# The experts stage of a four-layer kernel: last token group written out, end of the last unit reordered, two GpSimd steps moved

## The reference, cut to what matters

```python
logits = einsum('bsh,eh->bse', x, classifier_w)
probs  = softmax(logits)
idx    = top_k(probs + bias, 2);  rw = probs[idx] * 1.5
g = einsum('bsh,eih->bsei', x, gate_w)
u = einsum('bsh,eih->bsei', x, up_w)
act = silu(g) * u
out = einsum('bse,bseh->bsh', w_full[..., :8], einsum('bsei,ehi->bseh', act, down_w))
out = out + x * sum(w_full[..., 8:], axis=-1)
```

## Time and profile before

| | |
|---|---|
| median of 3 runs | 836.54 us |
| lowest and highest | 835.28 and 837.89 us |
| span of the profiled execution, first to last instruction | 832.7 us |
| that execution's own time | not given apart from its span; the median of the runs is 3.8 us above the span |
| first matmul of the experts' units, and first of the latent stage | 172.0 and 349.2 us |
| busy share of the span, TensorE, VectorE, ScalarE, GpSimd | 90%, 74%, 49%, 69% |

### The profile page before, as it was taken

The page is one execution under the profiler, slowest core; times in us unless marked ns, Lnnn a source line. Parts: engine busy times, 40 slices in busy tenths (PEclk is TensorE's granted clock), DMA queues, the critical chain, the costliest instruction groups (busy, mean ns, idle before and its releaser), DMA issues. The chain is left out here.

```text
span 832.7 us, 14911 instructions
## 1 busy us (share of the span) xinstructions
PE 750.6 (90%) x4808; PEld 535.8 (64%) x4808; DVE 615.8 (74%) x1115; ACT 406.6 (49%) x1084; POOL 570.9 (69%) x589
## 2 busy tenths in 40 slices
PE   4999999859999999689999999999999999866785
PEld 2555555447878877556777777777777777543454
DVE  5898999868887878665565576886678667749995
ACT  1688888533322322216454544555454445444453
POOL 5667776326676757564657778787878887716976
PEclk9999999989999999999999999999999999998999
DMA  9200000040000010122110000000000000000011
GB/s 262 103 1 0 0 0 1 2 168 20 20 19 20 19 57 0 57 95 96 48 49 1 1 1 1 3 1 1 1 1 2 1 2 1 1 2 7 25 33 38
DMA packets 8763, 24.12 MB, mean 29 GB/s; under 512 B 1711, under 2 KB 5167, under 8 KB 8087
## 3 DMA queue, kind: packets, MB, share of 16 engines
q1 hardware_dynamic: 8154, 23.28, 8.5%
q10 hardware_dynamic: 549, 0.08, 0.1%
HBM read 21.26 MB, written 2.10 MB: 28 GB/s over the span
## 5 line engine op out<-in xcount | busy, mean ns | idle before, releaser
L1606 POOL TENSOR_TENSOR q<-turned 64x512 f32<-64x512 f32 x128 | 168.0, 1313 | 23.5 <-DVE turned L1532 9.5
L1283 PE MATMUL ps<-l_yt,a 128*128 128x512 f32 x576 | 144.1, 400 | 2.1 <-ACT p L1429 1.6
L1283 PEld LDWEIGHTS ps<-l_yt,a 128*128 128x128 f32 x576 | 104.9, 188 | 26.9 <-issue 4.7
L1593 POOL TENSOR_TENSOR p<-p,l_inverse 128x512 f32<-128x512 f32 x64 | 66.8, 1047 | 77.3 <-DVE l_inverse L1554 76.9
L1429 ACT ACTIVATE p<-ps,l_negmax 128x128 f32<-128x128 f32 x256 | 91.1, 382 | 43.1 <-DVE l_negmax L1523 43.1
L1532 DVE TENSOR_TENSOR turned<-ps,rope 128x1024 f32<-128x1024 f32 x64 | 78.0, 1220 | 42.4 <-PE ps L1283 39.8
L871 PE MATMUL ps<-yt_experts,wsplit 128*128 (+1 forms) x384 | 97.3, 403 | 5.7 <-DVE h L974 5.2
L467 DVE TENSOR_REDUCE negmax<-ps 128x4 f32<-128x512 f32 x128 | 84.4, 685 | 13.3 <-PE ps L290 12.8
L871 PEld LDWEIGHTS ps<-yt_experts,wsplit 128*128 128x128 f32 x384 | 71.2, 192 | 23.1 <-issue 5.4
L1523 DVE TENSOR_REDUCE l_negmax<-ps 128x4 f32<-128x512 f32 x64 | 41.2, 686 | 45.8 <-PE ps L1341 45.6
L383 ACT ACTIVATE pt<-ps 128x512 f32<-128x512 f32 x128 | 71.2, 599 | 6.8 <-PE ps L312 4.5
(11 more groups left out here) (213 smaller groups left out, 1571.1 us busy)
## 6 DMA issues: line engine op xcount, KB each, us to landing
wide<-in_wide SPq DMA_DIRECT2D x8, 768.0 KB, 4.5
mx_raw<-in_mx SPq DMA_DIRECT2D x8, 384.0 KB, 3.1
x<-in_x SPq DMA_DIRECT2D x4, 512.0 KB, 8.4
ctx_t<-in_ctx_t SPq DMA_DIRECT2D x1, 2048.0 KB, 7.8
out<-x SPq DMA_DIRECT2D x16, 128.0 KB, 1.7
narrow<-in_narrow SPq DMA_DIRECT2D x8, 192.0 KB, 2.7
ktraw<-in_ctx_rows SPq DMA_DIRECT2D x1, 1248.0 KB
wraw<-in_gate SPq DMA_DIRECT2D x1, 1024.0 KB, 18.1
```

The lines of the kernel that those rows point to most:

```text
L1283: out = pe.matmul(tile_bank(n, k), a[i][:, pa, kin, k * 128:(k + 1) * 128], yt[j % 2][:, py, kin, :, :].rearrange("p b s -> p (b s)"), sta ...
L1593: pool.tensor_tensor(p[:, head, :, :], p[:, head, :, :], spread(inverse[:, head, :], 2, S), ALU.mult).then_inc(normed[head], 1)
L1606: t = pool.tensor_tensor(out[rows[(head + half) % 2], head, :], turned[rows[head], half, :], turned[rows[head], 2 + half, :], ALU.add)
```

## The change

It writes the last group out as code, with a loop over groups 1 and 2 only. In step 31 VectorE weighs unit 31 (`weigh`) before it quantises the last chunk. GpSimd finishes the last chunk one step later, behind the low part of unit 31, and TensorE's transposes of it come a step later, behind the last down products. The offset of the rows moves from x = 7 to x = 5 in every group. The means and variances of 12 sequences move into step 29, between up and down. The reciprocal deviations of the first four sequences move into step 30, and the other twelve to the latent stage. One step at the end falls away.

```diff
             group(0)
-            with engine.Fori(1, GROUPS) as j:
+            with engine.Fori(1, GROUPS - 1) as j:
                 group(j)
-            for x in range(3):
+            group(GROUPS - 1)
+            for x in range(2):
                 step(UNITS + x, GROUPS, x)
...
-                if x % 2 == 0 and inside(u - 2, UNITS):
+                if x % 2 == 0 and inside(u - 2, UNITS) and inside(u, UNITS):
+                    turn_quantised(u, 4 * j + x // 2, x)
+                if isinstance(u, int) and u == UNITS + 1:
+                    turn_quantised(UNITS, 2 * EXPERTS, 0)
...
-                if inside(u - 1, UNITS):
-                    dve.wait_ge(weight_spread, u)
-                    dve.wait_ge(inner_made, u)
-                    wait(dve, h_lo, u - 2)
-                    dve.tensor_tensor(h[old][:, :], inner[old][:, :], weight_ps, ALU.mult).then_inc(h_made, 1)
+                if inside(u - 1, UNITS) and inside(u, UNITS):
+                    weigh(u - 1, old)
+                if isinstance(u, int) and u == UNITS - 1:
+                    weigh(u, par)
...
                     (shift_up if x % 2 else block_powers)(u, j, x)
+                if isinstance(u, int) and u == UNITS - 3:
+                    mean_and_variance(dve, m, parts_made, stats_made, range(B - 4))
                 if x == 1 and inside(j - 1, GROUPS):
-                    if not inside(j, GROUPS):
-                        mean_and_variance(dve, m, parts_made, stats_made, range(B - 4))
...
-                if inside(u, UNITS) and x == 7:
+                if inside(u, UNITS) and x == 5:
                     pool.wait_ge(affine, j + 4)
...
-                    else:
-                        pool.wait_ge(mx_step, MX_STEPS * (c + 1))
-                        wait(pool, mx_turned, c - 1)
-                        pool.tensor_tensor(quantised[(x // 2) % 2][:, :].rearrange("p (n c) -> p n c", c=MX), chunk,
-                                           spread(scale[:, :], 2, MX), ALU.mult).then_inc(mx_made, 1)
+                    elif not isinstance(u, int) or u < UNITS - 1:
+                        finish_chunk(c, x)
+                if isinstance(u, int) and u == UNITS:
+                    finish_chunk(2 * EXPERTS - 1, EXPERTS - 1)
...
-                if inside(u, UNITS) and x in (3, 7):
+                if inside(u, UNITS) and x in (3, 5):
                     scale_x(j, x)
+                if isinstance(u, int) and u == UNITS - 2:
+                    pool.wait_ge(stats_made, B - 4)
+                    reciprocal_deviation(pool, m, var_made, slice(0, 4))
...
             steps(pool, step)
-            pool.wait_ge(stats_made, B - 4)
-            reciprocal_deviation(pool, m, var_made, slice(0, B - 4))
...
-                    reciprocal_deviation(pool, m, var_made, slice(B - 4, B))
+                    reciprocal_deviation(pool, m, var_made, slice(4, B))
```

More of the change, by code:

```diff
@@ L898, in step, with turn_quantised @@
                     t.then_inc(down_made, 1)
-                if x % 2 == 0 and inside(u - 2, UNITS):
[L900 to L908, removed]
+                if x % 2 == 0 and inside(u - 2, UNITS) and inside(u, UNITS):
+                    turn_quantised(u, 4 * j + x // 2, x)
+                if isinstance(u, int) and u == UNITS + 1:
+                    turn_quantised(UNITS, 2 * EXPERTS, 0)
+            def turn_quantised(u, c, x):
+                pe.wait_ge(mx_made, c)
+                wait(pe, mx_kept, c - 1)
+                if isinstance(u, int) and u in (2, 4):
+                    pe.wait_ge(w_lo, 2 + u // 2)
+                for i in range(3):
+                    t = pe.transpose(mx_ps[:, i * 128:(i + 1) * 128],
+                                     quantised[(x // 2 - 1) % 2][:, i * 128:(i + 1) * 128], m.ident16[:, :])
+                t.then_inc(mx_turned, 1)
             for b in range(B):
@@ L995, in step, with weigh @@
                         dve.bn_stats(m.parts[:, 4 * (j - 1) + s, :], m.x[:, 4 * (j - 1) + s, :]).then_inc(parts_made, 1)
+            def weigh(u, par):
+                dve.wait_ge(weight_spread, u + 1)
+                dve.wait_ge(inner_made, u + 1)
+                wait(dve, h_lo, u - 1)
+                dve.tensor_tensor(h[par][:, :], inner[par][:, :], weight_ps, ALU.mult).then_inc(h_made, 1)
             def mx_then(instruction, c, k, before):
@@ L1079, in step, with finish_chunk @@
                         pool.tensor_tensor(chunk, chunk, spread(inverse[:, :], 2, MX), ALU.mult).then_inc(mx_divided, 1)
-                    else:
-                        pool.wait_ge(mx_step, MX_STEPS * (c + 1))
-                        wait(pool, mx_turned, c - 1)
-                        pool.tensor_tensor(quantised[(x // 2) % 2][:, :].rearrange("p (n c) -> p n c", c=MX), chunk,
-                                           spread(scale[:, :], 2, MX), ALU.mult).then_inc(mx_made, 1)
+                    elif not isinstance(u, int) or u < UNITS - 1:
+                        finish_chunk(c, x)
+                if isinstance(u, int) and u == UNITS:
+                    finish_chunk(2 * EXPERTS - 1, EXPERTS - 1)
                 if inside(u, UNITS) and x < ROTARY_STEPS:
                     rotate_context(pool, m, rotated, j, x)
-                if inside(u, UNITS) and x in (3, 7):
+                if inside(u, UNITS) and x in (3, 5):
                     scale_x(j, x)
+                if isinstance(u, int) and u == UNITS - 2:
+                    pool.wait_ge(stats_made, B - 4)
+                    reciprocal_deviation(pool, m, var_made, slice(0, 4))
+            def finish_chunk(c, x):
+                chunk = raw[(x // 4) % 2][:, (x // 2) % 2, :].rearrange("p (n c) -> p n c", c=MX)
+                pool.wait_ge(mx_step, MX_STEPS * (c + 1))
+                wait(pool, mx_turned, c - 1)
+                pool.tensor_tensor(quantised[(x // 2) % 2][:, :].rearrange("p (n c) -> p n c", c=MX), chunk,
+                                   spread(scale[:, :], 2, MX), ALU.mult).then_inc(mx_made, 1)
             steps(pool, step)
-            pool.wait_ge(stats_made, B - 4)
-            reciprocal_deviation(pool, m, var_made, slice(0, B - 4))
 def rotate_context(pool, m, rotated, j, k):
```

## The result

The kernel after takes 831.32 us, the median of 9 runs (829.22 to 836.05), against 837.45 for the kernel before in 9 runs beside it (835.28 to 839.90). The ratio is 0.9931 [0.9916, 0.9946], so the change makes the kernel faster by 0.7%.

A forecast was written before the change was run, and what follows sets the result against it. It took the stage's end to be a relay of single engines, and VectorE to be held by GpSimd in units 9 and 25. Terms -3.0 + 0.9 - 2.6 - 0.8 = -5.5 gave 831.0 us, range 829.0 to 834.8.

The forecast's parts named there:

- End of the stage, -3.0: End of experts stage: earlier weighting of unit 31 and no offset between last low parts, -3.0 us (bounds -3.4, -0.9).
- Means and variances, +0.9: Step 29: twelve VectorE instructions between up and down stand on the path without cover, +0.9 us (bound 0).
- Offset, -2.6: Units 9 and 25: with the offset at x = 5 VectorE is no longer held, -1.32 us each, -2.6 together.
- no operation of VectorE on operands in the same memory runs beside one of GpSimd: Experts stage: VectorE and GpSimd exclude each other on the same memory, and the one starting second waits.
- The rival with the moved offset: At x = 5 the offset delays the powers past `inner` of x = 7, +5.2 us over four groups; 838.8 us, chance 0.06.
- Last group written out, -0.8: Step 24 and units 25 and 29: no back edge or register work, -0.3, -0.3 and -0.2 us.
- Deviations, 0: Step 30 and latent stage: the split reciprocal deviations fit into GpSimd's idle time, 0 us, bound +0.3.
- The sum: All terms together: -5.5 us, giving 831.0 us; this case had chance 0.52.
- I take the same 3.8 around its span: Whole kernel: the runs' median lies 3.8 us above the profiled span, taken as the profiled execution's excess too.
- the forecast span, 827.2: Whole kernel: the profiled span expected after the change, beside a forecast time of 831.0 us.
- whatever ends the stage earlier moves all that follows by as much: End of experts stage: the latent stage's start waits for every engine, so an earlier end shifts everything after equally.
- 1.3 of scatter: Forecast range: allowance for scatter between runs below the lowest and above the highest of the first three cases.

The follow-up runs named there:

- putting the offset back: Kernel after with the offset of the rows returned to x = 7 in groups 0 to 2, group 3 keeping x = 5; 834.18 us, ratio to before 0.9995.
- the last group alone: Kernel before with only its last group written out as code; 841.80 us, ratio to before 1.009.
- the means in step 30 and added products: Kernel after with means and variances moved to step 30 and 10 extra TensorE products in waits at the stage's end; 829.06 us, ratio to before 0.9922.
- the offset alone: Kernel before with only the offset of the rows moved from x = 7 to x = 5; 830.59 us, ratio to before 0.9946.
- the third group: Runs on the third chip; the unaltered kernel after, run there a third time, took 832.06 us, ratio 0.9955 to the kernel before (836.69).
- all written out: Kernel after with all four groups as code and means and variances in step 30; 830.47 us, ratio 0.9959; with 10 extra TensorE products 831.18 us.
- the means in step 30: Kernel after with means and variances of 12 sequences moved from step 29 to step 30; 828.96 us, ratio to before 0.9934.

## Why the prediction was right, point by point

- **End of the stage, -3.0:** right, -3.12. Counted from the first product of unit 31, the step said `h` at 5.05, the last low part done at 7.7, the addition at 11.2 and the copy at 11.6; measured are 5.06, 7.86, 10.98 and 11.49. The chunk that was pushed behind is late next: L1031 is held by the first low part (1.04) and L1032 by the second (1.33), L1033 and L1040 take 0.56, and the copy ends the stage behind the addition, all as the step had it.
- **Means and variances, +0.9:** right, +0.80. There was no cover, and a place one step later costs nothing.
- **Offset, -2.6:** right. Unit 9 to 11 gives -1.30; for unit 25 to 27 putting the offset back costs 1.21. L1031 started at 227.18, the last rotation piece had ended at 227.17. The step had 228.30 against 228.33. The two met within 0.01, and VectorE was not held, as in unit 17. The next meeting, of L1033 (227.96) with the low part (228.00), was as close; in the kernel before the low part had been first there (229.26 against 229.34). That it would fall this way was read from unit 17 and not worked out: 0.04 us decided in unit 9, and 0.10 in unit 25. The Trainium skill, "SBUF — State Buffer", section "Who interferes with whom", gives the ports to whichever starts first, for its whole instruction. The rows of after agree, on the other side this time: the low part that started 0.04 behind L1033 is held, 1.68. It is longer by 0.39 where L1033 had 0.52 left, so they show which of the two is held and not that it stands still all that time. The prediction's own words, that no operation of VectorE on operands in the same memory runs beside one of GpSimd, are too wide: in step 30 the reduction that opens the powers takes its usual 0.55 in the middle of the offset. The low part of unit 8 before, the reduction and the offset after:

```profile
229.26 1.29 POOL L1073 TENSOR_TENSOR ht<-h,ht 128x512 fp32r<-128x512 f32 x1 [0.17 <-POOL kvs L1107]
```

```profile
330.33 0.55 DVE L1022 TENSOR_REDUCE mx_scale<-mx_raw 128x12 f32<-128x384 f32 x1
```

```profile
329.96 1.90 POOL L1073 TENSOR_TENSOR x<-x,r_offset 128x1024 f32<-128x1024 f32 x1
```

- **The rival with the moved offset:** it did not come. 0.4 us of VectorE's idle were to be left before `inner` of x = 7; 0.45 are left before unit 23, at the place that the step counted, and 0.37, 0.43 and 0.35 before units 7, 15 and 31. The release is still TensorE's own product:

```profile
294.54 0.69 DVE L975 TENSOR_TENSOR inner<-gated,ps 128x512 f32<-128x512 f32 x1 [0.45 <-PE ps L872]
```

- **Last group written out, -0.8:** right in kind. Unit 24 gives -0.29 (-0.3), unit 25 -0.21 by the kernel with the last group alone (-0.3), and units 27 to 31, without the aggregation, -0.25 by the same kernel (-0.2). The three make -0.75; the 0.9% that this kernel lost in time lies at the end of its stage and behind it, with the clock. The gap of VectorE at step 24 is the exit's 0.31, where the back edge had 0.70:

```profile
299.35 0.69 DVE L975 TENSOR_TENSOR inner<-gated,ps 128x512 f32<-128x512 f32 x1 [0.31 <-DVE mx_raw L1042]
```

- **Deviations, 0:** right. The power of 4 columns ends at 335.74, the low part starts at 335.78. In the latent stage the longer power costs about 0.1: with the offset put back, where the clock at its head is 0.97 as in the kernel before, the second addition starts 19.18 us behind latent's first product (364.22 - 345.04), before 19.05.

```profile
364.22 5.24 POOL L1627 TENSOR_TENSOR q<-turned 64x512 f32<-64x512 f32 x4
```

- **The sum** of the stage was -5.5 and is -5.69, and the time, 831.32, lies 0.3 from the forecast. That the time came so close is in part luck. The stage gained 5.7 to 5.8 us in all three profiles of the kernel after, but its ratio to the kernel before was 0.9931, 0.9978 (interval up to 1.0008, which can't be told from no change) and 0.9955. Two steps around the sum failed. One is "I take the same 3.8 around its span": an execution of the kernel after takes 1.8 us more than its span (830.41 - 828.6), one of the kernel before 2.1. So the profiled execution of before was one of about 834.8, quicker than any that is listed of it beside the first result, and 0.3 of the gain in time lies outside of the span, for which the sum had no term. As the sum was set against the median the 3.8 did no harm to the time, but the forecast span, 827.2, is missed by 1.4. The other is that "whatever ends the stage earlier moves all that follows by as much": what follows is 486.3, 490.1 and 487.1 us long in the three profiles of the kernel after, and the "1.3 of scatter" of the range stands against 6.8 between the lowest and the highest of the 9 runs.

## What to carry to other kernels

A relay of several engines at the end of a stage is counted well from the rows of one profile: put what the others wait for first, and count what was pushed behind it. When two engines lock the same ports, a gap of some hundredths can decide on more than 1 us (here 0.04 on 1.3 us), so look in the profile for a pair that already met that closely and see who was held. A gain of half a percent should be read from the stage itself in both profiles, for the part behind it may move by as much on its own.

## What the runs showed of the hardware that was not expected

Behind the stage the same work takes between 482.8 and 490.6 us, and the difference goes with the clock that TensorE is granted. The busy time in three stretches (from the start of the latent stage: 35 us, 330 us, 120 us) of the kernel before; the columns are the stretch and its length, then busy time and instructions of PE, PEld, DVE, ACT and POOL, the granted clock, the DMA share and GB/s:

```profile
349.19:384.19 35.00, 28.85 (x168) 21.08 (x168) 23.41 (x42) 13.34 (x37) 16.68 (x17) 0.97 0.34 119
384.19:714.19 330.00, 329.70 (x2342) 246.40 (x2340) 222.11 (x361) 169.28 (x627) 253.33 (x214) 1.00 0.03 10
714.19:834.19 120.00, 83.18 (x597) 53.77 (x596) 88.82 (x150) 56.72 (x115) 78.77 (x50) 0.95 0.06 18
```

The same of the kernel after, in the first profile:

```profile
342.35:377.35 35.00, 29.78 (x158) 23.19 (x158) 20.34 (x36) 10.74 (x24) 15.71 (x14) 0.85 0.34 118
...
707.35:827.35 120.00, 86.03 (x611) 56.58 (x609) 91.43 (x153) 59.30 (x129) 80.54 (x52) 0.96 0.05 17
```

The same kernel once more:

```profile
345.06:380.06 35.00, 29.94 (x158) 23.31 (x158) 20.43 (x36) 11.06 (x25) 15.72 (x14) 0.85 0.34 118
...
710.06:830.06 120.00, 90.26 (x595) 58.50 (x595) 91.40 (x153) 58.11 (x126) 80.34 (x52) 0.89 0.05 16
```

And with the means in step 30 and added products:

```profile
341.04:376.04 35.00, 28.85 (x166) 22.07 (x168) 21.81 (x39) 13.35 (x37) 16.87 (x16) 0.95 0.34 118
...
706.04:826.04 120.00, 83.19 (x598) 54.96 (x596) 88.96 (x150) 56.72 (x115) 78.78 (x50) 0.95 0.06 19
```

In the middle stretch TensorE is busy 329.70 of 330 us at full clock. In the other two it waits in between, and in both the clock is at 1.2 GHz for part of the time: in the first 5 us of the latent stage the granted clock is 1.00 in the kernel before and 0.66 in the kernel after. Added up over the first and the last stretch, TensorE is busy 112.0 us in the kernel before and with the means in step 30 and products (latent-end 483.5 and 482.8), 115.8 in the kernel after (486.3) and 120.2 in its second profile (490.1). So the part behind the stage is longer as TensorE is longer busy with the same products. All fourteen profiles lie close to one line here, up to 120.8 us busy and 490.6 us in the last group alone (correlation 0.98). The moved deviations are not needed for it: the offset alone (488.2) and the last group alone (490.6) have the code of the kernel before behind the stage.

This is shown of the profiles, and the mean clock of each execution bears it out. Of the kernel after in the third group, six executions with 0.981 have spans of 827.1 to 829.4, and five with 0.975 have 831.1 to 834.5. What decides which of them an execution gets stays open. It is not chance alone: the kernel after has no more than 0.981 in any of its 31 executions, whereas the kernel before reaches 0.986 on each of the three chips and the offset alone has 0.983 to 0.986 in four of its five. But a changed stage moves it without a rule that these runs would show: the last group alone had 0.965 to 0.970 in each of its executions, all written out 0.973 to 0.979, the means in step 30 0.975 to 0.983.
